# Neighbour maxima folded bank by bank instead of reduced group by group, in a graph layer on one core

## The reference

```python
mask = A != 0
scores = jnp.where(mask, -jnp.arange(N), neg_inf)
vals, idx = jax.lax.top_k(scores, S)              # S = 25
feats = jnp.where(vals[..., None] > neg_inf, X[idx], neg_inf)
agg = feats.max(axis=2)
agg = jnp.where((mask.sum(-1) <= S)[..., None], jnp.maximum(agg, 0.0), agg)
h = jnp.concatenate([X, agg], axis=-1)
out = relu(h @ W + b)                             # W is 256 x 128
x = layernorm(x + out)                            # over the 128 features, no scale
```

## Time and profile before

| | us |
|---|---|
| median of 3 runs | 665.32 (660.34 to 666.41) |
| the profiled execution | 665.66 |
| its span, first to last instruction | 663.9 |
| PE busy | 531.7 |
| DVE busy | 493.4 |
| ACT busy | 397.9 |
| POOL busy | 306.5 |
| mean granted TensorE clock | 0.925 of 2.4 GHz |

### The profile page before, as it was taken

The page is one execution under the profiler, slowest core; times in us unless marked ns, Lnnn a source line. Parts: engine busy times, 40 slices in busy tenths (PEclk is TensorE's granted clock), DMA queues, the critical chain, the costliest instruction groups (busy, mean ns, idle before and its releaser), DMA issues.

```text
span 663.9 us, 14085 instructions
## 1 busy us (share of the span) xinstructions
PE 531.7 (80%) x4600; PEld 354.0 (53%) x4600; DVE 493.4 (74%) x1100; ACT 397.9 (60%) x762; POOL 306.5 (46%) x511
## 2 busy tenths in 40 slices
PE   4778999869877689949888698885987778994992
PEld 2355666447654466527655276553665356651762
DVE  4777898658885599937887478975898459992795
ACT  6824675448844588617784377744875358651554
POOL 4554455535256253552554445553525625455320
PEclk9989999969999799978998699996999969996997
DMA  7852445414365244732466244652446522021002
GB/s 249 196 154 79 111 116 137 125 57 114 77 164 135 70 114 90 179 92 70 111 166 137 53 102 113 171 130 66 108 75 169 130 71 49 3 65 41 14 19 64
DMA packets 84455, 69.52 MB, mean 105 GB/s; under 512 B 56291, under 2 KB 72934, under 8 KB 84326
## 3 DMA queue, kind: packets, MB, share of 16 engines
q1 hardware_dynamic: 77926, 54.93, 33.4%
q0 software_dynamic: 6400, 13.12, 6.9%
HBM read 50.99 MB, written 4.19 MB: 83 GB/s over the span
## 4 chain that ended last, share of the span: by engine, by line
PE 40%; DVE 23%; another core or an unknown queue 11%; issue 9%; ACT 9%; DVEq 6%; DMA 1%; POOL 0%; SPq 0%; ACTq 0%; POOLq 0%
PE pair L1183 32%; DVE part L865 12%; DVEq L973 4%; DVE hot L860 2%; PE p_V L1223 2%; PE p_V L1166 2%; PE misc L1228 2%; ACT mask L657 1%; ACT row_work L787 1%; ACT distance L700 1%; DVE agg_t L1015 1%; ACT hot L707 1%; DVE hot_high L860 1%; DMA adj_sb<-in_adj 1%
## 5 line engine op out<-in xcount | busy, mean ns | idle before, releaser
L1183 PE MATMUL pair<-hot,x_part 128*128 128x128 bf16 (+3 forms) x3120 | 424.0, 282 | 53.5 <-DVE part L865 34.2
L865 DVE TENSOR_REDUCE part<-pair 128x128 f32<-128x1024 f32 (+1 forms) x256 | 279.9, 1102 | 140.8 <-remote 70.5
L1183 PEld LDWEIGHTS pair<-hot,x_part 128*128 128x128 bf16 x3120 | 239.4, 99 | 170.5 <-issue 52.0
L508 POOL DMA_INDIRECT g_feat<-in_x,g_idx x200 | 196.1, 981 | 96.9 <-issue 85.2
L589 POOL TENSOR_TENSOR y_sb<-relu_sb,x_sb 128x128 f32<-128x128 f32 x64 | 30.0, 468 | 228.4 <-ACT relu_sb L718 227.9
L692 ACT ACTIVATE hot<-V,first_bias 128x1024 bf16<-128x1024 bf16 x56 | 64.0, 1142 | 94.3 <-remote 70.8
L664 ACT ACTIVATE V<-p_V 128x512 bf16<-128x512 f32 x98 | 57.6, 588 | 91.6 <-PE p_V L1166 49.4
L860 DVE TENSOR_SCALAR hot<-V 128x1024 bf16<-128x1024 bf16 x224 | 77.4, 367 | 0.0
L707 ACT ACTIVATE hot<-distance,one 128x1024 bf16<-128x1024 bf16 x56 | 63.9, 1142 | 0.2
L700 ACT ACTIVATE distance<-V,second_bias 128x1024 bf16<-128x1024 bf16 x56 | 63.7, 1137 | 0.0
L657 ACT ACTIVATE mask<-adj_sb 128x1024 bf16<-128x1024 uint32 x56 | 58.8, 1049 | 6.9 <-DMA adj_sb<-in_adj 6.5
(11 more groups left out here) (107 smaller groups left out, 446.5 us busy)
## 6 DMA issues: line engine op xcount, KB each, us to landing
adj_sb<-in_adj SPq DMA_DIRECT2D x56, 512.0 KB
g_adj<-in_adj SPq DMA_DIRECT2D x8, 512.0 KB
x_sb<-in_x SPq DMA_DIRECT2D x8, 512.0 KB
out<-y_sb SPq DMA_DIRECT2D x7, 512.0 KB
g_feat<-in_x,g_idx POOLq DMA_INDIRECT x200
maskT<-mask SPq DMA_TRANSPOSE x49
out<-y_sb SPq DMA_DIRECT2D x1, 256.0 KB
w_sb<-in_W SPq DMA_DIRECT2D x1, 128.0 KB, 6.2
```

Source lines behind the costliest of these rows:

```text
L508: pool.indirect_dma_start(out=g_feat[w][:, k, :], out_offset=None, in_=x_rows, in_offset=bass.IndirectOffsetOnAxis(ap=g_idx[w][:, k:k + 1] ...
L865: dve.tensor_reduce(part[:, par(q, s), :, p], slots_of(q, s, p).rearrange("f k i -> f i k"), AX.X, ALU.max).then_inc(s_used, 1)
L1183: last = pe.matmul(dst, x_part[:, q, part_no, kb], one_hot, start=(first and part_no == 0), stop=(final and part_no == PARTS - 1))
```

## The change

- ScalarE copies group 0 (one bank) into `kept`, 128 x 512 fp32, behind `first_rank`.
- VectorE folds each bank of the later groups into `kept` with an elementwise maximum: `fold_low`, then the one-hots of that gap, then `fold_high`. It no longer reduces over slots.
- The merge of the groups becomes two smaller maxima, `halve` (4 slots to 2) and `merge` (2 to 1), in the next step, with one-hots between.
- TensorE: `count` stands behind group 0 instead of group 1; the linear layer of the tile before stands behind group 3 instead of group 2. The bias product comes first in it, with 128 rows, 125 of them zeros, instead of 3.
- ScalarE: `copy_xt` stands ahead of the mask, `normalise` ahead of copy_V half 1.

```diff
-            def reduce_group(i, q, s, p):
+            def fold_low(i, q, s, p):
                 dve.wait_ge(s_pair, pair_no(i, q, s, p) + 1)
-                dve.tensor_reduce(part[:, par(q, s), :, p], slots_of(q, s, p).rearrange("f k i -> f i k"),
-                                  AX.X, ALU.max).then_inc(s_used, 1)
+                if p == 1:
+                    dve.wait_ge(s_kept, pos(i, q, s) + 1)
+                else:
+                    dve.wait_ge(s_used, fold_no(i, q, s, p))
+                maxima = kept[:, par(q, s)]
+                dve.tensor_tensor(maxima, slots_of(q, s, p)[:, 0:BANK], maxima, ALU.max).then_inc(s_low, 1)
+            def fold_high(i, q, s, p):
+                dve.wait_ge(s_low, fold_no(i, q, s, p) + 1)
+                maxima = kept[:, par(q, s)]
+                dve.tensor_tensor(maxima, slots_of(q, s, p)[:, BANK:2 * BANK], maxima, ALU.max).then_inc(s_used, 1)
...
+            def halve(i, q, s):
+                dve.wait_ge(s_used, fold_no(i, q, s, COUNT[s]))
+                dve.wait_ge(s_xdone, redo_no(i, q, s) + (2 if s == MT else 1))
+                dve.tensor_tensor(maxima[:, 0:2], maxima[:, 0:2], maxima[:, 2:4], ALU.max).then_inc(s_half, 1)
             def merge(i, q, s):
...
+                dve.tensor_tensor(agg_t[:, par(q, s)], maxima[:, 0], maxima[:, 1], ALU.max).then_inc(s_agg, 1)
...
                     for p in range(COUNT[s]):
-                        reduce_group(i, q, s, p)
-                        if p == 0:
-                            if s > 1:
-                                merge(i, q, s - 1)
...
+                        if p > 0:
+                            fold_low(i, q, s, p)
+                        elif done:
+                            halve(*done)
+                        if p < gaps and nxt:
+                            one_hots(*nxt, ...)
+                        if p > 0:
+                            fold_high(i, q, s, p)
+                        elif done:
+                            merge(*done)
```

ScalarE:

```diff
+            def keep_first(i, q, s):
+                m = pos(i, q, s)
+                act.wait_ge(s_pair, pair_no(i, q, s, 0) + 1)
+                if m > 1:
+                    act.wait_ge(s_agg, m - 1)
+                nc.scalar.activation(kept[:, par(q, s)], slots_of(q, s, 0), ACT.Copy).then_inc(s_kept, 1)
...
                         first_rank(*nxt)
+                    keep_first(i, q, s)
+                    if nxt:
                         second_distance(*nxt)
...
                         second_rank(*nxt)
+                    if s in TURNS:
+                        copy_xt(i, q, TURNS[s])
                     if to_mask:
                         make_mask(*to_mask)
                     if s > 1:
                         relu(i, q, s - 1)
-                    if s in TURNS:
-                        copy_xt(i, q, TURNS[s])
...
+                    if s in (6, 7) and not is_first(i, q):
+                        normalise(2 * i + q - 1, pq, range(4 * (s - 6), 4 * (s - 5)))
                     if to_rank:
                         copy_V(*to_rank, 1)
-                    if s in (6, 7) and not is_first(i, q):
-                        normalise(2 * i + q - 1, pq, range(4 * (s - 6), 4 * (s - 5)))
```

TensorE:

```diff
-                    pe.wait_ge(s_used, pair_no(i, q, s, p) - since_last_use(q, s, p) + 1)
+                    j, r, t, g = last_use(i, q, s, p)
+                    if g == 0:
+                        pe.wait_ge(s_kept, pos(j, r, t) + 1)
+                    else:
+                        pe.wait_ge(s_used, fold_no(j, r, t, g) + 1)
...
-            def linear(xt, agg, signal):
-                pe.matmul(p_out, xt, w_sb[:, 0], start=True, stop=False)
-                pe.matmul(p_out, agg, w_sb[:, 1], start=False, stop=False)
-                pe.matmul(p_out, ones_row[:, :], bias_bf[:, :], start=False, stop=True).then_inc(signal, 1)
+            def linear_begin(xt):
+                pe.matmul(p_out, ones_row[:, :], bias_bf[:, :], start=True, stop=False)
+                pe.matmul(p_out, xt, w_sb[:, 0], start=False, stop=False)
+            def linear_end(agg, signal):
+                pe.matmul(p_out, agg, w_sb[:, 1], start=False, stop=True).then_inc(signal, 1)
...
                     pick_group(i, q, s, 0)
+                    if s > 1 and to_rank:
+                        out_free(i, q, ORDER[s - 1])
+                        count(*to_rank)
                     if to_rank and not late:
                         rank_product(*to_rank, 0)
                     pick_group(i, q, s, 1)
-                    if s > 1 and to_rank:
-                        out_free(i, q, ORDER[s - 1])
-                        count(*to_rank)
                     pick_group(i, q, s, 2)
-                    if s > 1:
-                        linear_main(i, q, s - 1)
...
                     if COUNT[s] > 3:
                         pick_group(i, q, s, 3)
+                    if s > 1:
+                        linear_main(i, q, s - 1)
```

79 lines of the change are left out of this document (45 added, 34 removed).

## The result

The changed kernel takes 680.73 us in the median of 10 runs (667.62 to 689.8), the kernel before 665.25 (660.34 to 668.38, 10 runs). The forecast was 685.6 us, or +3.0%: the median has 15.5 of the 19.9 us that it added, the ratio a third of them. The profiled execution of the kernel before took 665.66 us, so the two traces have 16.8 us between them. That this lies near 19.9 is luck, for hardly one of the large terms came out as forecast.

What follows compares the result with a forecast made beforehand. No engine bounds the whole; in steps 4 to 7 three engines run almost in step. The sum was 665.7 + 1.8 + 1.4 + 18.6 - 2.3 + 0.4 = 685.6 us, with 8 in 10 from 648 to 702.

Steps and rivals of the forecast that it cites:

- the residual's gap: Step 2: tile 1's later relu moves GpSimd's residual, ahead of step 3's six gathers; 0 to +3 us, taken as 0.
- the loop of step 5 into 6: ScalarE's relu, row work and copy before TensorE's rank product; -0.3 to +1.9 us a batch, taken as +0.5.
- the differences under 1%: Whole kernel: a change within 6.7 us can't be told from none; chance 0.17.
- The folds: VectorE's maxima replacing reductions: 0.69 us per fold of 512 columns, 0 us a step, bounds -0.5 and +0.5.
- Linear late: Linear behind group 3 makes ScalarE's relu-to-copy loop close late for TensorE's rank product; 3.1 us a batch, +18.6 us, chance 0.55.
- if the blocks are shorter or gone: Sign on the seven stretches behind step 2, expected as long as before: gathers' order against TensorE's small matmuls would matter most.
- Releasing PSUM: Groups 2 of steps 3 and 4: two folds free a PSUM pair later than one reduction; one place counted, +1.8 us.
- the level: The batch's level comes some 0.25 us later, behind group 4's one-hots and second fold; +0.2 x 7 = +1.4 us.
- the tail: End of the kernel: it gets one fold more, +0.4 us.
- the wait for agg_t: TensorE's linear waits 7.3 us in 9 places; six are counted under the late linear, the others give -2.3 us.

## Why the prediction was wrong, step by step

The forecast's terms against the two traces, in us:

```
                                  forecast   measured
steps 5 to 7, batches 1 to 6         +17.4      +44.0
step 1, batches 1 to 6                +0.3       -6.5
steps 2 to 4, batches 1 to 6          +1.8      -32.5
batch 0, batch 7, tail                +0.4      +11.7
sum                                  +19.9      +16.7
```

Two terms failed above all: the residual's gap, taken at 0, which gave some 25 us back, and the loop of step 5 into 6, taken at +0.5 us a batch, which cost 4.6. They nearly cancel. Where TensorE's signals come in time there is no such gain, and the same change costs 6.4%, twice the forecast. By its ratio of 1.0094 the result lies among the differences under 1%, of which the prediction said that they can't be told from none, and to which it gave 0.17.

**The folds: right.** 0.687 us for 0.69. At 0 us a step with bounds of 0.5, steps 5 came out at -0.4, steps 3 and 4 at -0.2 and steps 6 at -0.1, as seen with the linear early in the prompt condition. A fold that needs the one before it starts 0.04 us behind its end, and independent one-hots start 0.08 us ahead of a fold's end. The Trainium skill's formula (VectorE: DVE Perf Modes, The TRN2 errata) gives 0.691 for this fold, and the trace agrees. Its rule that a fixed latency lies exposed between instructions, which small ones pay each time, agrees only where the second needs the first, and at 0.04 us.

**Linear late: the right mechanism, under-sized.** The path from relu to copy to rank product is what the chip does, 2.29 us for 2.28, and step 5 grows by 1.0 us late and 1.1 prompt for 1.2. The step that failed here is "between -0.3 and +1.9; I take +0.5" for step 5 into 6. It costs 1.8 us a batch in the prompt condition (1.4 in most) and 4.6 in the late one, where the linear's signal comes 2.2 to 2.5 us late among four gathers. The prediction had that hold-up in its sentence ("behind a relu that the same gathers can hold up") and priced it by a wait that was already there. It should have added the two: the linear late means that its signal falls among the gathers, which it didn't before (19 late signals of the linear in the changed kernel, 2 in the one before). Steps 5 to 7 of batches 1 to 6 cost 44.0 us against 17.4 forecast (6 x 2.9); in the prompt condition 32.9 (6.4, 10.8 and 15.7), with the coupling through tile 0's maxima in step 7 in it.

**Batch 0: left out.** "In the batches that have both rank products and row work, 1 to 6" excluded it. It costs 10.5 us here and 6.5 in the prompt condition. Of the latter, 4.0 is step 7, which the late linear alone also costs 3.2, and 2.8 is step 2 behind the extra ranks, which the folding kernel with the linear early also has (2.3).

**The residual's gap: this is the step that failed.** The prediction had seen that a late relu of tile 1 moves the residual and the six gathers of step 3 ("so 0 to +3; I take 0, since TensorE gets forward in that gap"). It happened in four of seven batches instead of two. And it isn't a cost: steps 2 and 3 take 23.2 to 24.0 us in these four and 29.1 to 30.3 in the other three, 6.1 us less on the means (23.65 against 29.8), some 25 us in all. That is most of step 3's -27.8, and it offsets the under-sized loops and batch 0. Why a shorter run of gathers relieves TensorE's signals stays open (below). The bounds of this term were one-sided. The prediction named the sign under "what would show it" ("if the blocks are shorter or gone, the gathers' order against TensorE's small matmuls matters more than any of this") and gave it no chance and no price.

**Releasing PSUM, the level, the tail: small.** No run isolates the +1.8 us for the release of PSUM. In the traces TensorE's matmuls of the groups wait less for VectorE's release, 15.0 us in 4 places for 34.2 in 19, and steps 3 and 4 of batches 1 to 6, where the term was placed, are shorter. The tail was 0.8 for 0.4. The level's late place was priced at 0.2 x 7 = 1.4 us with the copy; the edit that moves it recovers 5 us in the prompt condition. Step 1 as a whole was nevertheless 6.5 us shorter here, which fits the wait for agg_t that is gone; that the two belong together isn't shown.

**What is shown and what isn't.** Shown by runs, in the prompt condition: the late linear's place is the loss (1.069 alone, 1.008 when undone, 1.0636 for the whole), its loop through ScalarE closes (10 to 15 us less when ScalarE's row work is taken out of it), the level's place is worth some 5 us to the folding kernel, and with the level first the folds are worth nothing. In the late condition, that of the result, the linear back behind group 2 was run only with other edits beside it (0.9882 with the level first, 1.0227 with the folds adjacent), and the late linear alone not at all, so the account there rests on the two traces. Seen only in traces: that a pause between two bursts of gathers relieves the late signals. It rests on 4 batches with a pause of 3.56 us or more against 31 with one of 0.64 (before 7, changed 3, and 21 of three folding kernels in the late condition), which took 29.1 to 31.3 us without exception. The wait that would have tested it met the prompt condition every time. The kernel before with the level first has three relieved batches with unparted gathers, so there is another way to it, which I can't name. The changed kernel's runs scatter over 22 us, those of the kernel before with the level first over 16.5, the kernel before's over 8. That fits batches that are relieved or not from run to run, and the 12 us by which the traced execution lies above those in the ratio are the worth of two such batches; only one run of each has a trace, so it stays a guess. The same guess would explain why the ratio is a third of the forecast. What makes a chip or a session late rather than prompt is open.

## What to carry to other kernels

When an instruction is moved, follow its signal, not only its own time: list who waits for it on each engine, what stands behind that waiter, and price each loop that closes through it, every one that the trace of before shows at zero too. A stretch that looks fixed because nothing of the change touches it may be fixed only by the order of two other things; if the change can move one of them, the term has a gain side and needs a bound there. And where a second loss sits beside the first, measure the change once without it: beside a stall of 118 us that the change partly removed, 0.9% was left to see of a loss of 6.4%.

## What the runs showed of the hardware

TensorE's signals come late in some sessions and not in others, and mostly while GpSimd issues indirect DMAs: in the trace of before 57 of 69 late group signals have a gather running between the matmul's end and the signal, in the changed kernel's 44 of 53. In the late condition a linear that ended at 137.27 reached ScalarE at 140.56, with six gathers just finished, and folds waited up to 11.7 us for groups. The same kernel in the prompt condition, in the same place:

```profile
193.76 0.39 PE L1279 MATMUL misc<-w_sb,agg_t 128*128 128x128 f32 x2
194.19 0.28 ACT L737 ACTIVATE relu_sb<-misc 128x128 f32<-128x128 f32 x1 [1.09 <-PE misc L1279]
194.43 0.95 POOL L519 DMA_INDIRECT g_feat<-in_x,g_idx  x1 [0.30 <-issue]
```

Here the relu starts 0.04 us behind the linear's end, among the gathers, and no signal of a group or of the linear in the prompt traces is over 0.5 us late. For the kernel before, the whole difference is worth 118 us of 665: the busy times differ little (TensorE 531.7 and 496.4 us, VectorE 493.4 and 494.1, the second of each from the prompt trace with the wait that held nothing), while VectorE is busy 74% of the one span and 91% of the other:

```profile
PE 496.4 (91%) x4600; PEld 344.2 (63%) x4600; DVE 494.1 (91%) x1100; ACT 398.0 (73%) x762; POOL 305.8 (56%) x511
```

The granted TensorE clock goes with it, 0.925 of 2.4 GHz on the mean in the late trace and 0.97 to 0.99 in the prompt ones; the block's window shows 0.80 where TensorE was busy for 3.91 of 11.5 us. Part of TensorE's extra 35 us may be its clock; no run separates it.
